# Routed experts of a mixture layer: dense over all tokens, or on gathered tiles of 128 tokens

## The reference, cut to what matters

```python
E, K, F = (8, 2, 352)          # experts, chosen per token, width
SCALE = 2.5
scores = jax.nn.softmax(x @ gate_w.T, axis=-1)
topk_w, topk_i = jax.lax.top_k(scores, K)
topk_w = topk_w / (topk_w.sum(-1, keepdims=True) + 1e-20) * SCALE
combine = jnp.zeros((T, E)).at[jnp.arange(T)[:, None], topk_i].set(topk_w)
g = jax.nn.silu(jnp.einsum('td,edf->etf', x, w_gate)) * jnp.einsum('td,edf->etf', x, w_up)
expert_out = jnp.einsum('etf,efd->etd', g, w_down)
y = jnp.einsum('te,etd->td', combine, expert_out)
return y + silu(x @ sw_gate) * (x @ sw_up) @ sw_down    # shared expert, width 704
```

## Time and profile before

| | |
|---|---|
| median of three runs | 1431.11 us |
| the profiled execution, its own time | 1430.48 us |
| its span, from the first to the last instruction | 1428.7 us |
| PE busy | 1299.7 us, 91% of the span |
| DVE, ACT, POOL busy | 51%, 42%, 36% |
| mean granted TensorE clock | 0.95 of full |
| mixture, from its first `moe_GU` matmul (978.8) to its end (1242.0) | 263.2 us |

### The profile page before, as it was taken

How to read it: one execution, slowest core, us unless ns; L and a number is a source line. 1 busy time by engine, 2 the same in 40 slices (tenths; PEclk the granted TensorE clock), 3 DMA queues, 4 the chain that set the end, 5 groups by cost and what they waited for, 6 DMA issues and landing times. The chain is left out here.

```text
span 1428.7 us, 33786 instructions
## 1 busy us (share of the span) xinstructions
PE 1299.7 (91%) x14368; PEld 1145.5 (80%) x14368; DVE 733.6 (51%) x1149; ACT 600.3 (42%) x958; POOL 514.7 (36%) x505
## 2 busy tenths in 40 slices
PE   5799999999999999999999878677999999877689
PEld 4789998999898989989998667345888888766578
DVE  5565466557555764665573427445223233564632
ACT  4555555555555555555555122334433333211300
POOL 4643233234323432332341005623654544254400
PEclk9999999999999999999999559997999999989989
DMA  6855764757475657656563202003110100014035
GB/s 187 192 138 124 162 146 117 150 123 167 99 179 132 144 118 167 141 126 142 127 141 77 64 22 90 1 0 119 43 52 32 62 11 0 0 30 174 1 139 205
DMA packets 51618, 148.05 MB, mean 104 GB/s; under 512 B 23752, under 2 KB 28184, under 8 KB 49432
## 3 DMA queue, kind: packets, MB, share of 16 engines
q1 hardware_dynamic: 50328, 144.99, 40.8%
q10 hardware_dynamic: 1152, 1.05, 0.2%
HBM read 62.29 MB, written 1.31 MB: 45 GB/s over the span
## 5 line engine op out<-in xcount | busy, mean ns | idle before, releaser
L366 ACT ACTIVATE xa_pt<-xa_sc 128x1024 f32<-128x1024 f32 (+1 forms) x224 | 212.6, 964 | 149.6 <-PE xa_sc L558 149.6
L412 DVE TENSOR_REDUCE xa_mx<-xa_sc 128x2 f32<-128x804 f32 x256 | 243.5, 992 | 41.2 <-PE xa_sc L542 40.9
L558 PE MATMUL xa_sc<-xa_queries,xa_keys 104*128 104x128 f32 (+1 forms) x1664 | 232.3, 285 | 2.2 <-DVE xa_queries L427 1.8
L558 PEld LDWEIGHTS xa_sc<-xa_queries,xa_keys 104*128 104x128 f32 (+1 forms) x1664 | 206.5, 195 | 20.9 <-issue 8.1
L1153 PE MATMUL moe_GU<-moe_lnH,moe_gu 128*128 128x512 f32 (+1 forms) x480 | 154.8, 401 | 6.8 <-DVE moe_h L1301 4.4
L479 PE MATMUL xa_pj<-xa_ctx_hi,xa_wk 128*128 128x400 f32 (+1 forms) x512 | 156.9, 348 | 0.9 <-DVE xa_qst L440 0.9
L479 PE MATMUL xa_pj<-xa_wv,xa_ctx_hi 128*128 128x256 f32 (+1 forms) x832 | 155.3, 286 | 0.1
L542 PE MATMUL xa_sc<-xa_keys,xa_queries 96*128 96x402 f32 x512 | 137.7, 371 | 13.3 <-DMA xa_keys<-xa_kst_hi 7.6
L300 POOL TENSOR_TENSOR xa_kst_lo<-xa_wk,xa_kst_hi 128x400 fp32r<-128x400 f32 x64 | 67.3, 1052 | 226.3 <-ACT xa_kst_hi L345 226.3
L569 PE MATMUL xa_op<-xa_pt,xa_values 128*32 128x64 f32 x6656 | 141.1, 228 | 7.7 <-ACT xa_pt L366 3.3
L295 POOL TENSOR_TENSOR xa_ctx_lo<-xa_raw,xa_ctx_hi 128x1600 fp32r<-128x1600 f32 (+1 forms) x32 | 116.0, 3625 | 78.0 <-DVE xa_ctx_hi L405 75.3
(11 more groups left out here) (244 smaller groups left out, 2041.6 us busy)
## 6 DMA issues: line engine op xcount, KB each, us to landing
xa_keys<-xa_kst_hi SPq DMA_DIRECT2D x256, 200.2 KB, 6.0
xa_keys<-xa_kst_lo SPq DMA_DIRECT2D x128, 200.2 KB, 5.2
xa_raw<-in_ctxT SPq DMA_DIRECT2D x15, 1601.0 KB, 8.8
gf_w<-in_gf_w SPq DMA_DIRECT2D x16, 1024.0 KB, 7.2
moe_gu_raw<-in_moe_gu SPq DMA_DIRECT2D x10, 704.0 KB, 4.1
moe_dn_raw<-in_moe_down SPq DMA_DIRECT2D x10, 384.0 KB, 3.1
xa_queries<-xa_qst SPq DMA_DIRECT2D x96, 32.0 KB, 3.4
X<-in_x SPq DMA_DIRECT2D x1, 1024.0 KB, 5.8
```

The lines of the kernel that those rows point to most:

```text
L366: nc.scalar.activation(PT[ptslot(step)][0:rows, 0:nt], SC[bank(step)][0:rows, 0:nt], ACT.Exp, scale=float(D0) ** -0.5).then_inc(ex_done, 1)
L412: nc.vector.tensor_reduce(mx[:, u // 2, 2 * (u % 2):2 * (u % 2) + 2], SC[bank(step)][:, :, 0:MXN], AX.X, ALU.max).then_inc(mx_done, 1)
L558: last = mm(SC[bank(step)][0:rows, kk, a * P:(a + 1) * P], KS[:, 2 * a + h, kt * P:kt * P + rows], QS[b % 2][:, 2 * a + h, :], start=True, ...
```

## The change

Only the two halves of the shared expert still run over all tokens, with the same split matmuls. The eight routed experts run on the tokens that chose them:

1. DVE gives each of the 2048 (token, choice) pairs a place. The places of one expert begin at a multiple of 128, so there are at most 16 + 7 = 23 tiles of 128 places (`NT`). PE helps with prefix sums (`prefixes`).
2. POOL scatters the rows of the normalised input y to the places in an HBM buffer `XG` with 16 indirect DMAs of 128 rows (128 KB). It was filled with zeros by a DMA in `layer_norm(1)`.
3. For each tile SP loads 128 rows to one of three buffers XS. PE transposes them (xt), DVE copies them to SBUF, PE multiplies by the weights of the tile's expert (up: 4 matmuls of 352 columns), ACT and DVE make h, PE transposes it (ht), ACT copies it, PE multiplies by the down weights (dn: 3 matmuls of 256 columns), ACT copies the result to YS and SP stores it to the HBM buffer `YG`. These matmuls are in plain f32, not split. All eight experts' weights lie in one SBUF tile `ex`; PE loads the column offset of the tile's expert from SBUF to a register (`value_load`).
4. After all stores have landed, POOL gathers each token's two rows with 16 indirect DMAs, and DVE adds them to X with their weights.

Beside this: the shared halves' weights are split during `layer_norm(2)`; the loads of `mc` and `sb` weights move from `layer_norm(2)` to `layer_norm(3)`, because `ex` takes the room; six of the eight routed experts are loaded in `layer_norm(1)`, the other two in `experts`; both self attentions share one set of semaphores, which POOL clears in `layer_norm(4)` (28 instructions); bias rows use the semaphore of their weights.

The core of the diff (the arithmetic of the places, the renamed semaphores and the arrays on the host are left out):

```diff
+WE = 2 * CH * FE + 3 * D
+NT = (T * P * TOPK) // P + NE - 1
+NXS, NYS, NYG = 3, 2, 4
...
+    loads = [(gate[:], w["gate"], w_in), (mc[:], w["consts"], w_in)]
+    loads += [(gu[j], w["sgu"][j], w_in) for j in range(2)] + [(dn[j], w["sdown"][j], w_in) for j in range(2)]
+    loads += [(XG.rearrange("(i p) d -> p i d", p=P), w["zero"].unsqueeze(1).to_broadcast([P, NT, D]), w_in)]
+    routed = [(ex[:, e * WE:(e + 1) * WE], w["ex"][e], w_in) for e in range(NE)]
+    loads += routed[:NE - 2]
...
+def shared_splits(nc, ctx, buffers):
...
+    def high(act):
+        act.wait_ge(w_in, loaded)
+        for part, raw in parts:
+            nc.scalar.activation(part[0][:], raw, ACT.Copy).then_inc(hi, 1)
+
+    def low(pool):
+        for n, (part, raw) in enumerate(parts):
+            pool.wait_ge(hi, n + 1)
+            nc.gpsimd.tensor_tensor(part[1][:], raw, part[0][:].bitcast(f32), ALU.subtract).then_inc(lo, 1)
...
+def expert_order():
+
+    shared = lambda s, lo, hi: [("su", s, n) for n in range(lo, hi)]
+    down = lambda s: [("sd", s, n) for n in range(ND)]
+    o = shared(0, 0, NU) + shared(1, 0, 1) + down(0) + shared(1, 1, NU)
+    o += [("xt", 0, 0), ("xt", 1, 0), ("up", 0, 0)]
+    for i in range(NT + 1):
+        o += [("xt", i + 2, 0)] * (i + 2 < NT) + [("up", i + 1, 0)] * (i + 1 < NT)
+        o += [("ht", i, 0)] * (i < NT) + [("dn", i - 1, 0)] * (i > 0)
+    return o + down(1)
...
         @block.sync
         def _(sp):
-            def load(e, j):
-
-                ge(sp, gu_lo, e - 1)
-                sp.dma_start(gu_raw[j][:], w["gu"][e]).then_inc(gu_in[j], 16)
-                ge(sp, dn_lo, e - 1)
-                sp.dma_start(dn_raw[j][:], w["down"][e]).then_inc(dn_in[j], 16)
-
-            with sp.Fori(1, NX // 2) as i:
-                load(i * 2, 0)
-                load(i * 2 + 1, 1)
+            sp.wait_ge(w_lo, 4)
+            for dst, src, counted in last_experts:
+                sp.dma_start(dst, src).then_inc(counted, 16)
+            sp.wait_ge(scattered, 16 * 2 * T)
+            for i in range(NT + NXS):
+                if i < NT:
+                    if i >= NXS:
+                        sp.wait_ge(xt_full, i - NXS + 1)
+                    sp.dma_start(XS[i % NXS][:], XG[i * P:(i + 1) * P]).then_inc(xs_in[i % NXS], 16)
+                n = i - NXS
+                if n >= 0:
+                    sp.wait_ge(y_ev, n + 1)
+                    sp.dma_start(YG[n * P:(n + 1) * P], YS[n % NYS][:]).then_inc(y_out[n % NYS], 16)
...
+                if k == "xt":
+                    pe.wait_ge(xs_in[i % NXS], 16 * (i // NXS + 1))
...
+                elif k == "sd":
+                    if n == 0:
+                        pe.wait_ge(hlo_done[i], NU)
...
+                elif k == "up":
+                    if i == 0:
+                        pe.wait_ge(placed, 2)
+                        pe.wait_ge(w_in, loaded + 16 * len(last_experts))
+                    at = pe.value_load(at_[0:1, i:i + 1], min_val=0, max_val=(NE - 1) * WE)
+                    where.append(at)
+                    pe.wait_ge(xt_ev, i + 1)
+                    for q in range(CH):
+                        for x in range(2):
+                            last = mm(GU[(nth(*step) - 1) % 2][:, x, 0:FE], XT[i % 2][:, q, :],
+                                      ex[:, bass.ds(at + (q * 2 + x) * FE, FE)], start=q == 0, stop=q == CH - 1)
...
+                elif k == "dn":
+                    pe.wait_ge(ht_ev, i + 1)
...
+            pool.wait_ge(placed, 1)
+            for t in range(T):
+                for k in range(2):
+                    nc.gpsimd.indirect_dma_start(out=XG, out_offset=bass.IndirectOffsetOnAxis(ap=idx[:, k, t:t + 1], axis=0),
+                                                 in_=y[:, t], in_offset=None).then_inc(scattered, 16)
+            for j in range(NYS):
+                pool.wait_ge(y_out[j], 16 * len(range(j, NT, NYS)))
+            for t in range(T):
+                for k in range(2):
+                    nc.gpsimd.indirect_dma_start(out=back[2 * t + k], out_offset=None, in_=YG,
+                                                 in_offset=bass.IndirectOffsetOnAxis(ap=idx[:, k, t:t + 1], axis=0)).then_inc(gathered[t * NYG // T], 16)
...
-        layer_norm(nc, 2, ln, X, stats, lnT, c, loads=loads_mc + row_load_mc + loads_sb + row_load_sb)
-        experts(nc, "moe", X, stats, lnT, c, moe, expert_parts)
+        layer_norm(nc, 2, ln, X, stats, lnT, c, also=splits[3], y=y)
+        experts(nc, "moe", X, y, stats, lnT, c, expert_parts, splits)
```

More of the change, by code:

```diff
@@ L585, with layer_norm @@
 LN_SEMS = ("stat", "var", "std", "norm", "tr", "ev_dve", "ev_act")
-def layer_norm(nc, k, sems, X, stats, lnT, c, loads=(), also={}):
+def layer_norm(nc, k, sems, X, stats, lnT, c, loads=(), also={}, y=None):
     ctx = ExitStack()
@@ L1053, in expert_buffers @@
[L1053 to L1058, removed]
+    sb = lambda n, s: ctx.enter_context(nc.sbuf_tensor(f"moe_{n}", s, f32))
+    ex, gate, mc = sb("ex", [P, NE * WE]), sb("gate", [P, CH, NE]), sb("consts", [P, 2 * P + NT])
+    raw = [ex[:, (NE - 2 + j) * WE:(NE - 1 + j) * WE] for j in range(2)]
@@ new lines @@
+UNITS = [(f, g) for f in range(3) for g in range(2)]
+NU, ND = len(UNITS), T // 2
+def expert_order():
[7 more added lines that the diff above has]
+    return o + down(1)
@@ L1060, in experts @@
+def experts(nc, tag, X, y, stats, lnT, c, buffers, splits):
     ctx = ExitStack()
@@ L1107, in over_splits @@
-        def over_splits(eng, units, split_gu, split_dn, then=lambda: None):
-            def two(i, last=False):
-                for j in range(2):
-                    e = i * 2 + j
-                    units(e, j)
-                    if not (last and j == 1):
-                        split_dn(e + 1, 1 - j)
-                    if not last:
-                        split_gu(e + 2, j)
-            split_gu(0, 0)
-            split_gu(1, 1)
-            split_dn(0, 0)
-            then()
-            two(0)
-            with eng.Fori(1, NX // 2 - 1) as i:
-                two(i)
-            two(NX // 2 - 1, last=True)
+        RT = ctx.enter_context(nc.psum_tensor(f"{tag}_RT", [P, 512], f32))
@@ L1303, in add @@
-            def add(e, j):
-                for n in range(ND):
-                    dve.wait_ge(dn_full, e * ND + (n + 1))
+            step_(V.tensor_reduce(m8[:], LG, AX.X, ALU.max))
+            step_(V.tensor_tensor(lg[:], LG, over8(m8[:]), ALU.subtract))
+            for step in order:
+                k, i, n = step
+                if k in ("su", "up"):
+                    multiplied(step)
+                    before = unit_before(step)
+                    if before and before[:2] == ("su", 1):
+                        lower_part(before[2])
+                elif k == "sd":
+                    dve.wait_ge(dn_full, nth(*step))
@@ L1480, in program @@
         ln = {n: ctx.enter_context(nc.semaphore(f"ln_{n}")) for n in LN_SEMS}
+        att = {n: ctx.enter_context(nc.semaphore(f"att_{n}")) for n in ATTENTION_SEMS}
         c, at = {}, 0
```

483 lines of the change are left out of this document (310 added, 173 removed).

## The result

The changed kernel takes 1471.42 us (median of four runs, 1467.75 to 1473.82), the kernel before 1430.80 (1430.29 to 1432.84): 1.0279 times as long, 95% interval 1.0252 to 1.0306. The forecast was 1470. The profiled execution took 1473.29 us, its span is 1471.5 (before 1428.7), so 42.8 us are to be explained: 24.2 lie ahead of the mixture's first `moe_GU` matmul, 16.6 in the mixture (279.8 in place of 263.2), 2.1 behind it.

What follows compares the result with a forecast made beforehand. The prediction took the old mixture stage to be bound by PE's matmul count. 1430.48 + 8.2 ahead of the mixture + 31.6 in it = 1470.3, so 1470 us; 8 in 10 range 1412 to 1522.

Steps and rivals of the forecast that it cites:

- shared halves: Start of the mixture: two up, one down and the units of the second half on PE, 46.5 us.
- 19 stalled rounds: Routed part, loads of tiles 4 to 22: PE waits for each load, 10.1 us a round, 191.9 us.
- rest to the last dn: End of the routed part: last up, last h and three dn with their waits, 9.9 us.
- tail: After the last dn: last store lands, sixteen POOL gathers of 20.8 us, last additions on DVE; mixture ends at 294.8.
- What bounds the rounds: Routed rounds: each tile load stands behind a store, so PE idles; 8.1 us a round at full clock.
- The break-even round of 8.0 us: Routed rounds: the round length at which the changed kernel would take as long as the kernel before.
- The clock: Routed rounds: PE's clock falls after pauses in four of five rounds, 2.5 us each, 2.0 on average.
- The register load: Each routed round, after the transposes: PE waits 0.8 us for the weight offset, bounds 0.1 and 1.7.
- SP's issues in `layer_norm(1)`: End of that block: eight added DMA issues at 0.55 each, covered by nothing, +4.4 us.
- the price of POOL's work: In layer_norm(2): four added subtractions on POOL take 10.0 us; first moe_GU comes 3.8 us later.
- POOL's DMAs: Scatter and gather of the mixture: sixteen indirect DMAs each, 1.3 us apiece, 20.8 a series.
- rival (d): Scatter and gather: POOL's indirect DMAs cost 3.0 us each, adding 54, for 1524 us; chance 0.16.

Runs made afterwards that it cites:

- e1_store_lag: Changed kernel with SP storing the result of tile i-4, not i-3, behind the load of tile i: 1376.06 us, 0.9609 of the kernel before.
- e4_filled: Changed kernel with 16 unneeded identity transposes ahead of each stalled wait for an input tile: 1445.47 us, 1.0097 of the kernel before.
- e5_no_register: Kernel of e1_store_lag with a constant weight column offset per tile in place of the register load: 1370.99 us, 0.9557 of the kernel before.
- e2_zero_in_sa: Changed kernel with only the filling of XG moved from layer_norm(1) to the self attention sa: 1461.59 us, 1.0203 of the kernel before.

## Why the prediction was right, and where it was not

The total was right within 1.4 us, the steps far less so. In the table (us) rows with a plus sign, and the last two, are changes against the kernel before; "shared halves", "first input tile" and "first dn" are times counted from the first `moe_GU` matmul; the others are durations.

| term | forecast | measured |
|---|---|---|
| `layer_norm(1)` | +4.4 | +13.8 |
| `layer_norm(2)` to the first `moe_GU` | +3.8 | +8.8 |
| shared halves done, from there | 46.5 | 49.4 |
| first input tile in | 49.5 | 51.4 |
| first dn done | 64.7 | 66.2 |
| 19 stalled rounds | 191.9 | 179.3 |
| rest to the last dn | 9.9 | 6.9 |
| tail | 28.3 | 27.3 |
| mixture | 294.8 | 279.8 |
| behind the mixture | 0 | +2.1 |
| ahead of `layer_norm(1)` | 0 | +1.6 |

- **What bounds the rounds: right.** Nineteen rounds wait at L1262 for a load that stands behind a store; e1_store_lag shows that this order is the whole cause. The round at the full clock was forecast at 8.1 us and is 8.0: the pause 3.0 (forecast 2.9), the register load 0.3 (0.8), all else 4.7 (4.35), since in a stalled round PE also waits for the steps between its transposes and `moe_GU`. Two misses of 0.4 to 0.5 us cancel in it.
- **The break-even round of 8.0 us: wrong.** It rested above all on the 8.2 us ahead of the mixture, which were 24.2. e4_filled has rounds of 8.0 us and is still 1.0% slower than the kernel before (13 us). By the measured times it is 9.44 - 40.6/19 = 7.3 us, and at that 19 x (8.0 - 7.3) gives the 13 us of e4_filled.
- **The clock: right in kind, a fall priced too high.** I took a fall in 4 of 5 rounds at 2.5 us. 15 of 19 rounds (4 of 5) fell, and the average of these is 9.82 in place of 8.03: 1.8 a fall. The 2.5 came from a stretch of 5.1 us of low clock in a dense stage; a round has less work than that to slow down. Fifteen falls at 1.8 are 27 us, where 19 x 2.0 = 38 were forecast; that is 11 of the 12.6 by which this term was too long.
- **The register load: mis-sized.** 0.8 forecast; 0.3 idle in a stalled round, and 4 to 5 us in the whole program without stalls by e5_no_register.
- **SP's issues in `layer_norm(1)`: mis-sized, the largest miss ahead of the mixture.** I priced eight issues at 0.55 and named the filling of `XG` in brackets, with no number. Its own issue took 0.66 us; the issue behind it took 9.94. That is all of the missing 9.4 us: with the filling moved, e2_zero_in_sa is 9.8 us faster.
- **`layer_norm(2)`: the price of POOL's work was right (10.2 us, forecast 10.0), its victim wrong.** I let DVE and the transposes run beside it. DVE was shut out, and its last copy ended after POOL. Then the 32 gate matmuls ran at the low clock (6.97 us, 4.26 before), behind a PE that had waited:

```profile
996.15:1002.90 6.75, 6.75 (x32) 6.75 (x32) 2.36 (x2) 3.26 (x3) 0.00 (x0) 0.50 0.86 321
```

- **POOL's DMAs: right.** 1.3 forecast, 1.35 and 1.28 measured; rival (d) was wrong.
- **The shared halves: 2.9 short.** The wait of the first down for h's low part was forecast at 2.2 us and is 2.54. What I left out are the prefix sums on PE, 18 small matmuls that stand from 1019.20 to 1021.38 and hold up everything behind them:

```profile
1019.20 0.44 PE L1226 MATMUL moe_RT<-moe_t,moe_consts 128*128 128x72 f32 x2
1019.48 1.90 PE L1228 MATMUL moe_RT<-moe_t,moe_consts 128*128 128x64 f32 x16
```

- **Behind the mixture: 2.1 instead of 0.** After 21.3 us of PE's idling in the tail come only 4 us of transposes before `mean_context`, and its first matmuls run at a clock of 0.50: four take 2.04 us where the earlier trace rows has 1.10.

The misses in the two layer norms (+14.4) and in the mixture (-15.0) cancelled; the +2.1 and +1.6 make up most of the 3.0 by which the profiled execution is above the forecast. The forecast of 1470 was in part luck; what it had right was the mechanism and its sign.

## What to carry to other kernels

When a dense stage becomes a chain through HBM, read the issuing engine's list first: a load that stands behind a store of the newest result turns transfer latency into a pause each round, here 3 us and, in 15 of 19 rounds, 1.8 more by the clock, and one step more between them was worth 95 us. Ahead of a barrier, don't price DMAs by their count or bytes alone: look at what the DMA just ahead of each issue is, and keep one like the filling of `XG` (2944 rows of 1 KB) where nobody waits for the issuing engine. After combining repairs look at the trace again: two that gave 95 and 14 us apart made a new stall of 8 to 10 us together.

## What the runs showed of the hardware that I had not expected

- An issue by SP right behind the filling of `XG` (2944 rows of 1 KB, HBM to HBM) blocks for 9.94 us in the changed kernel, for 9.2 to 10.6 in the other executions with both in `layer_norm(1)`, and for 8.4 to 9.1 in those with the issue in `sa`; six issues of 1.1 MB each, with rows of 8.7 KB, take 3.68 together.
- While POOL runs tensor_tensor from SBUF, DVE's tensor_scalar from SBUF to SBUF does not get on: eight of them take 11.33 us in place of 2.67.
- A register load in PE's list costs nothing in most rounds if PE has work in hand, 0.3 us of idle time if PE has just been released from a wait.
- During sixteen indirect DMAs of POOL, DVE can stand still for 7 to 9 us, and ACT for some 10 to 12 after its input is ready, with no releaser on the core. Its condition is open.
